# A four-layer network on one core: the last expert mixture as one stage, and the third attention's query rotation split

## The reference

```python
q_nope = (q_c @ W_uq)...            # q_c = q @ W_dq
q_rope = _rope(q_c @ W_qr)
scores = (einsum(q_nope, k_nope) + einsum(q_rope, k_rope)) * scale
scores = where((k_ids <= seg_id) & (k_ids >= seg_id - 8), scores, NEG)
attn = softmax(scores); out = (attn @ v) @ W_o
```

```python
scores = sigmoid(xt @ gate_w.T)                  # 8 experts
top_scores, top_idx = top_k(scores, 2)
top_scores = 2.5 * top_scores / (top_scores.sum() + 1e-20)
y[e] = (silu(xt @ w1[e]) * (xt @ w3[e])) @ w2[e]  # hidden width 176
out = sum of the chosen two, weighted, + (silu(xt @ sw1) * (xt @ sw3)) @ sw2
```

## Time and profile before

| | us |
|---|---|
| median of 3 runs (2387.63 to 2402.3) | 2391.42 |
| the profiled execution | 2387.03 |
| its span | 2385.2 |
| third attention, first rotary add to the last tile | 747.4 to 1231 |
| gate, first DMA issue | 1997.4 |
| routing | 2033 to 2057 |
| scatters | 2058.6 to 2139.3 |
| first routed unit | 2157.1 |
| first read of the results (L3018) | 2341.9 |
| PE, DVE, ACT, POOL busy, share of the span | 81%, 66%, 41%, 50% |

### The profile page before, as it was taken

One profiled execution on the slowest core, in us unless ns is written; L12 is line 12 of the kernel. 1 busy time (PEld: TensorE's weight loads), 2 busy tenths in 40 slices (PEclk: granted clock), 3 DMA queues, 4 the chain that ended last, 5 costly groups with the idle time before them and its releaser, 6 DMA issues. The chain is left out here.

```text
span 2385.2 us, 46698 instructions
## 1 busy us (share of the span) xinstructions
PE 1920.2 (81%) x16094; PEld 1429.0 (60%) x16128; DVE 1568.5 (66%) x3473; ACT 984.2 (41%) x2503; POOL 1184.3 (50%) x1523
## 2 busy tenths in 40 slices
PE   6979744796914888888868996799999997379995
PEld 5869421674714777777756664366666663247773
DVE  7956721765596999999955455688788873533336
ACT  3732311242234555555532222376666664123331
POOL 4720046532384666666642323388777872362331
PEclk8989756898966999999989998699999998679997
DMA  7721055505650000000000000444444433132336
GB/s 208 250 65 48 10 162 125 182 6 145 80 143 1 0 0 0 0 0 0 0 1 1 1 1 7 119 107 107 102 105 104 108 76 83 47 107 75 107 107 227
DMA packets 155592, 179.90 MB, mean 75 GB/s; under 512 B 39452, under 2 KB 136908, under 8 KB 150796
## 3 DMA queue, kind: packets, MB, share of 16 engines
q1 hardware_dynamic: 145596, 155.33, 24.4%
q0 software_dynamic: 9808, 22.20, 3.1%
HBM read 117.55 MB, written 59.33 MB: 74 GB/s over the span
## 5 line engine op out<-in xcount | busy, mean ns | idle before, releaser
L2712 DVE TENSOR_REDUCE mx<-bank 128x2 f32<-128x512 f32 x512 | 321.4, 680 | 91.2 <-PE bank L2574 91.1
L2678 ACT ACTIVATE e<-bank 128x512 f32<-128x512 f32 x512 | 269.5, 606 | 136.5 <-PE bank L2594 136.4
L2506 POOL TENSOR_TENSOR es<-e 128x256 f32<-128x256 f32 x384 | 271.2, 729 | 92.6 <-ACT e L2678 92.0
L2574 PE MATMUL bank<-k,q 72*128 72x256 bf16 x1024 | 205.4, 285 | 33.7 <-DMA k<-k_parts 33.5
L1859 POOL TENSOR_TENSOR q_l<-q_l,rot_l 64x512 f32<-64x512 f32 x128 | 162.3, 1268 | 127.6 <-DVE rot_l L2056 127.6
L2594 PE MATMUL bank<-q,k 74*128 74x256 bf16 x1024 | 196.8, 276 | 6.2 <-DMA q<-rows 3.6
L2574 PEld LDWEIGHTS bank<-k,q 72*128 72x128 bf16 x1024 | 92.4, 100 | 95.7 <-issue 48.5
L2611 PE MATMUL bank<-e,val 128*32 128x256 f32 x2048 | 140.5, 392 | 3.1 <-ACT nd L2673 0.6
L3036 POOL DMA_INDIRECT y<-y,got x71 | 69.0, 972 | 130.9 <-DVE y L3152 125.8
L3081 PE MATMUL bank<-w,hT 88*128 (+1 forms) x412 | 112.8, 398 | 24.3 <-ACT hT L3106 24.3
L1891 PE MATMUL bank<-qcT,wq_abs 96*128 96x128 f32 x1024 | 124.0, 280 | 0.0
(11 more groups left out here) (433 smaller groups left out, 5115.4 us busy)
## 6 DMA issues: line engine op xcount, KB each, us to landing
q<-q_parts SPq DMA_DIRECT2D x32, 576.0 KB
k<-k_parts SPq DMA_DIRECT2D x96, 192.0 KB
got<-rows SPq DMA_DIRECT2D x71, 128.5 KB, 2.1
rows<-no_row SPq DMA_DIRECT2D x1, 9088.0 KB
moe_rows<-zero_a SPq DMA_DIRECT2D x16, 512.0 KB, 3.2
w<-in_e0w SPq DMA_DIRECT2D x16, 512.0 KB, 3.6
parts_y<-y SPq DMA_DIRECT2D x32, 256.0 KB, 4.6
k_parts<-k_parts_a SPq DMA_DIRECT2D x96, 64.0 KB, 2.1
```

The lines of the kernel that those rows point to most:

```text
L2506: nc.gpsimd.tensor_tensor(es[:, n, :], e[:, n, 0, :], e[:, n, 1, :], ALU.add).then_inc(s["sum_ready"], 1)
L2574: last = nc.tensor.matmul(scores(r)[:, qt * D:(qt + 1) * D], q[0:R, b, h * D + qt * P:h * D + qt * P + P], k[0:R, b, h * D:(h + 1) * D], s ...
L2678: nc.scalar.activation(e[:, slot(i, r), :, :].rearrange("p k n -> p (k n)"), scoresT(r)[:, :], ACT.Exp).then_inc(s["exp_ready"], 1)
L2712: v.tensor_reduce(mx[:, a.n, 0, at:at + 2], scores(r)[:, :].rearrange("p (a n) -> p a n", a=2), AX.X, ALU.max, negate=True).then_inc(s["ma ...
```

## The change

In the third attention, `q_ready` rises after each four heads, and `rope` can do some of the quarters: the first quarter of the next tile stands between the two `sums`, the other three behind the second. Those who need all heads wait for the fourth quarter.

In the think stage the fill of `rows3` goes, with its two buffers.

The last mixture becomes one stage, `stage_l3_moe`. The 24 shared units come in eight groups of three (PER = 3), and each group also carries four tiles through the gate and the routing. A tile is normalized once, into a ring of 20 buffers (RING = 5 groups); that buffer feeds both the transposes and both scatters, and ACT's second copy goes. PE adds the counts of a group by eight small bf16 matmuls (`rank`), and a running `base` on DVE takes the place of the scan. Each expert has an area of fixed place in `rows3` (AREA3 = 4224 rows), so a token's row is known once its group is counted. `choose` and `place` are 24 DVE instructions a group. After the last group, `tables` (20 instructions) works out the expert and the first row of each of the 71 row tiles. SP then stores one tile of padding at the end of each expert's area, at an address from a register. Each read of a row tile takes its address from a register too. Rows carry one more number, the lower of the token's two experts, and two small DVE instructions per routed unit work out the home in `y3`; the weights are worked out in `shares` before the routed units. SiLU and sigmoid now alternate on ACT within one block. The weights are loaded with the shared expert's first.

```diff
@@ stage_l1_think
-        no_row = sb("no_row", [P, D]); no_home = sb("no_home", [P, T3])
...
-            sp.wait_ge(s["t_no_row"], 2)
-            empty = c.rows3.rearrange("(n p) d -> p n d", p=P)
-            sp.dma_start(empty[:, :, 0:D], no_row[:, :].unsqueeze(1).broadcast_to([P, T3, D])).then_inc(s["t_filled"], 16)
-            sp.dma_start(empty[:, :, D:D + 1], no_home[:, :].unsqueeze(2),
-                         allow_slow_non_contiguous=True).then_inc(s["t_filled"], 16)
...
@@ stage_l2_attention
                 for h in range(H2):
                     last = nc.tensor.matmul(bank(j, h // 4)[:, (h % 4) * P:(h % 4 + 1) * P], wq[:, h, :],
                                             qcT[:, j, :], start=True, stop=True)
-                last.then_inc(s["q_ready"], 1)
+                    if h % 4 == 3:
+                        last.then_inc(s["q_ready"], 1)
...
-            def rope(t, j):
-
-                dve.wait_ge(s["q_ready"], ready(t))
+            def rope(t, j, some=range(4)):
+
                 dve.wait_ge(s["scores_ready"], halves(t - LANES, 1))
-                for m in range(4):
+                for m in some:
+                    dve.wait_ge(s["q_ready"], quarters(t, m))
...
-                for n in range(2):
-                    sums(t, j, n)
-                rope(t + 1, 1 - j)
+                sums(t, j, 0)
+                rope(t + 1, 1 - j, range(1))
+                sums(t, j, 1)
+                rope(t + 1, 1 - j, range(1, 4))
                 back(t, j)
@@ stage_l3_moe, the SP queue
+            sp.dma_start(wg[:, :, :], c.d["g3w"].rearrange("(k p) n -> p k n", p=P)).then_inc(s["g3_loaded"], 16)
...
+            sp.wait_ge(s["w3_loaded"], 96)
+            sp.wait_ge(s["tables_ready"], 1)
+            for e in range(E3):
+                at = nc.values_load(base_i[0:1, e:e + 1], engines=(mybir.EngineType.SP,), min_val=0, max_val=E3 * AREA3 - P)
+                sp.dma_start(c.rows3[bass.ds(at, P), :], pads[:, e, :]).then_inc(s["pads_out"], 16)
+            sp.wait_ge(s["spare_out"], 32)
+            sp.wait_ge(s["pads_out"], 16 * E3)
+            for j in range(RING):
+                sp.wait_ge(s[sent_out[j]], 16 * TOP3 * WIDE * len(range(j, GR, RING)))
             for n in range(T3):
+                at = nc.values_load(at_row_i[0:1, n:n + 1], engines=(mybir.EngineType.SP,), min_val=0,
+                                    max_val=E3 * AREA3 + (SPARE - 1) * P)
                 wait(sp, y_out[n % GOT], 16 * (n // GOT))
-                sp.dma_start(got[:, n % GOT, :], c.rows3[n * P:(n + 1) * P, :]).then_inc(s[got_in[n % GOT]], 16)
+                sp.dma_start(got[:, n % GOT, :], c.rows3[bass.ds(at, P), :]).then_inc(s[got_in[n % GOT]], 16)
@@ GpSimd
+            for i in range(GR):
+                pool.wait_ge(s["sent_ready"], i + 1)
+                for t in tiles(i):
+                    for k in range(TOP3):
+                        nc.gpsimd.indirect_dma_start(
+                            out=c.rows3[:, :], out_offset=bass.IndirectOffsetOnAxis(ap=pos3[:, t, k:k + 1], axis=0),
+                            in_=sent[:, slot(t), :], in_offset=None, oob_is_err=True, bounds_check=E3 * AREA3 - 1,
+                        ).then_inc(s[sent_out[i % RING]], 16)
@@ TensorE
+            early_features(0)
+            early_features(1)
+            logits(0)
+            turn_scores(0)
+            pe.wait_ge(s["w3_shared"], 48)
+            for u in range(FIRST):
+                i, m = u // PER, u % PER
+                if m == 0 and i + 2 < GR:
+                    early_features(i + 2)
+                hidden(u)
+                if m == 1 and i + 1 < GR:
+                    logits(i + 1)
+                if u >= 1:
+                    turn(u - 1)
+                if m == 1:
+                    rank(i)
+                if m == 2 and i + 1 < GR:
+                    turn_scores(i + 1)
+                if u >= 2:
+                    down(u - 2)
+            turn(FIRST - 1)
+            down(FIRST - 2)
+            pe.wait_ge(s["w3_loaded"], 96)
+            pe.wait_ge(s["tables_ready"], 1)
@@ ScalarE
+            for u in range(FIRST):
+                i, m = u // PER, u % PER
+                if m == 0 and i + 2 < GR:
+                    early_copies(i + 2)
+                sigmoid(u)
+                if m == 1 and i + 1 < GR:
+                    score(i + 1)
+                if u >= 1:
+                    copy(u - 1)
@@ VectorE
+            for u in range(FIRST):
+                i, m = u // PER, u % PER
+                product(u)
+                if m == 0:
+                    choose(i)
+                if m == 1:
+                    place(i)
+                if m == 2 and i + 3 < GR:
+                    norms(i + 3)
+                if u == FIRST - 1:
+                    tables()
+                if u >= 2:
+                    finish(u - 2)
+            finish(FIRST - 2)
+            shares()
```

More of the change, by code:

```diff
@@ L2757, in _, with stage_l3_moe @@
             stats(end)
[L2760 removed]
+def stage_l3_moe(nc, c):
     with ExitStack() as ctx:
         sb = lambda n, sh, dt=F32: ctx.enter_context(nc.sbuf_tensor(n, sh, dt))
[L2764 to L2783, removed]
[L2784 to L2862 removed]
@@ L2982, in stage_l3_experts @@
         gates = lambda u: c.bank[u % 2]
-        turned = lambda u: c.bank[2 + u % 2][0:HH3, 0:2 * P]
+        turned = lambda u: c.bank[2 + (u % 2 if u > FIRST else 0)][0:HH3, 0:2 * P]
+        out = lambda u: c.bank[6 + u % 2 if u >= FIRST else 7][:, 0:D]
+        early = lambda t: c.bank[4 + t % 2][:, 0:D]
         feat = lambda n: c.bank[4 + n % 2][:, 0:D]
-        out = lambda u: c.bank[6 + u % 2][:, 0:D]
+        logitsT = c.bank[6][0:E3, :]
+        scores = c.bank[3][:, 0:WIDE * E3]
+        counts = c.bank[3][:, 64:64 + (WIDE + 1) * E3].rearrange("p (a e) -> p a e", e=E3)
+        slot = lambda t: t % (RING * WIDE)
+        tiles = lambda i: range(WIDE * i, WIDE * i + WIDE)
+        some = lambda i: slice(WIDE * i, WIDE * i + WIDE)
         ot = c.d["out"].rearrange("(n p) d -> p n d", p=P)
@@ L3064, in turn @@
                 pe.wait_ge(s["hid_ready"], u + 1)
-                wait(pe, "hT_ready", u - 1)
+                wait(pe, "hT_ready", u if u <= FIRST else u - 1)
                 for n in range(2):
@@ L3097, in _, with early_copies, score @@
         def _(act):
+            def early_copies(i):
+                for t in tiles(i):
+                    act.wait_ge(s["feat_read"], t + 1)
+                    act.copy(xT3[:, t, :], early(t)).then_inc(s["feat_copied"], 1)
+            def score(i):
+                act.wait_ge(s["logit_ready"], i + 1)
+                wait(act, "score_turned", i - 1)
+                nc.scalar.activation(scoreT[:, i % 2, :], logitsT, ACT.Sigmoid).then_inc(s["score_ready"], 1)
             def sigmoid(u):
@@ new lines, in norms, with choose @@
+            def norms(i):
+                if i >= RING:
+                    dve.wait_ge(s[sent_out[i % RING]], 16 * TOP3 * WIDE * (i // RING))
+                for t in tiles(i):
+                    v.tensor_scalar(sent[:, slot(t), 0:D], c.x[:, t, :], c.mean[:, t:t + 1], c.rstd[:, t:t + 1],
+                                    ALU.subtract, ALU.mult).then_inc(s["xn_ready"], 1)
+            def choose(i):
+                dve.wait_ge(s["score_turned"], i + 1)
+                ch.link(v.tensor_copy(cand[:, some(i), 0:E3], scores.rearrange("p (t e) -> p t e", e=E3)))
+                for t in tiles(i):
+                    last = v.max(top[:, t, :], cand[:, t, 0:E3])
+                ch.link(last)
+                ch.link(v.memset(top[:, some(i), TOP3:8], BIG))
+                for a, t in enumerate(tiles(i)):
+                    last = v.match_replace(out=left[:, a, :], in_to_replace=top[:, t, :], in_values=cand[:, t, :],
+                                           imm_value=-BIG)
+                ch.link(last)
+                v.tensor_tensor(mask_b[:, i % 2, :, :], left[:, :, 0:E3], cand[:, some(i), 0:E3],
+                                ALU.not_equal).then_inc(s["chosen_ready"], 1)
+                ch.link(v.tensor_tensor(mask[:, some(i), :], left[:, :, 0:E3], cand[:, some(i), 0:E3], ALU.not_equal))
```

427 lines of the change are left out of this document (198 added, 229 removed).

## The result

| | before | after |
|---|---|---|
| median of 15 runs each, us | 2391.63 (2386.21 to 2402.3) | 2409.08 (2402.2 to 2417.52) |
| ratio to before, 95% interval | | 1.0072, 1.0057 to 1.0086 |
| profiled execution, us (span) | 2387.03 (2385.2) | 2405.14 (2403.3) |

The change costs 17.5 us where 20 us less were forecast. The time lies beyond the range too. The mixture gained what was promised, and a little more; the attention lost three times what was promised.

A forecast was written before the change was run, and what follows sets the result against it. One core, barriered stages; in the third attention PE and DVE, each 88% busy, share the limit. Mixture -39, attention +19, fill 0 make -20 us: from 2391.4 to a forecast of 2371 us, 8-in-10 range 2345 to 2400.

The forecast's parts named there:

- Second sum and second turn: Third attention: their starts, forecast at 2.17 and 4.26 us after T0, the end of the first half's reciprocal.
- Nothing among them shrinks: turn to scores stays 5.90 us: Third attention, PE: second turn, both reads, projection and next scores keep their old pace, so scores start at T0+10.16.
- First half's scores: Third attention: 32 matmuls of about 1.1 us plus 0.1 hand-over to DVE, so the mask starts at T0+11.36.
- Mask to sum: Third attention: 3.22 us from mask to first exponent's end, so the first sum starts at T0+14.60; step 15.50 us.
- The bounds of the attention, -20 to +28: Around +19 us: -20 if PE's later turn is fully hidden, +28 if nothing is, with 0.3 us more latency per step.
- rival (c): Mixture: merged loop stays slow on PE's clock, slower by over 1% from a 17 us group; chance 0.11.
- Quarter signals: Third attention: signalling by quarters costs three more semaphore events on PE; no time was counted for them.
- The fill: Think stage: removing the 9.3 MB fill counts 0 us, with bounds 0 and -3 us.
- The front of the mixture: Mixture, stage start to first routed matmul: 159.7 us shortened by 39, bounds -45 and -31, at 11.6 us a group.
- the 3 us for it: Mixture: PE, idle some 15 us, starts the routed units at the lower clock level, costing 3 us.
- Rival (a): Third attention: rotation free through the projection's 1.4 us slack (chance 0.14), or gaining 0.66 us per step (0.10).
- Table loads bind: Mixture: ACT's two added table loads per group, 1.28 us each, forecast as hidden, would set the pace; chance 0.12.

The follow-up runs named there:

- e4: The changed kernel with seven more matmuls on PE in each attention step, in the gap before the second turn; 2398.54 us, 0.9952 of before.
- e3: The changed kernel with only DVE's old order put back (both sums, then the four rotations), quarter signals kept; 2365.79 us, 0.9820 of before.
- e6: The kernel before, unchanged, run again for a second profile; the median of before in its group was 2395.42 us.
- e5: The kernel after, unchanged, run again in another group; 2407.76 us, 1.0053 of before.
- e7: The changed kernel with only one of the first quarter's three rotation instructions between the two sums; 2324.45 us, 0.9707 of before.
- e10: e7 with SiLU in place of the sigmoid in the mixture's routing score; no total time given, its mixture front takes 132.6 us.
- e9: The changed kernel with two of the first quarter's three rotation instructions between the two sums; 0.9901 of before.
- e8: The changed kernel with the last four heads of the next tile's queries moved into PE's gap before the second turn; 2373.48 us, 0.9919 of before.
- e2: The changed kernel with the attention's functions of before; 2367.74 us, 0.9842 of before.
- e12: e7 once more, unchanged, in a later group; 2349.93 us, 0.9754 of before.

## Why the prediction was wrong

Term by term, with the forecast's numbers first.

- **Second sum and second turn**, T0+2.17 and 4.26: 2.18 and 4.27. Right.
- **"Nothing among them shrinks: turn to scores stays 5.90 us"**: 7.24. This is the step that failed. The durations of before were taken as fixed, but they were those of a PE that sat idle for 0.42 us before that turn, at a grant near 1 (0.98 over the stage, 1.00 from 790 to 1190). The edit's own delay made a hole of 2.00 us, and the turn and reads behind it ran at grants of 0.50 and 0.63. That is 1.34 us a step, 40 us in all. e4, with the hole filled, shows the 5.90 again.
- **First half's scores, 1.20 us to the mask**: 1.39 (1029.42 to 1030.81). Another 0.19, 6 us.
- **Mask to sum**, 14.60 - 11.36 = 3.24 us: 1034.04 - 1030.81 = 3.23. Right. With 1.34 and 0.19 on top of 15.50 the sum gives 17.03; this step is 17.05 (1034.96 - 1017.91).
- **The bounds of the attention, -20 to +28**: the upper one allowed 0.3 us of latencies and no change of clock, so the measured +63 was outside. Even the upper bound, with the mixture as measured, would have given a time inside the range. The forecast did treat the clock, as rival (c), but in the mixture, where the grant was low already (0.70), and not in the attention, where it was 0.98 and the change was about to make a hole.
- **Quarter signals**, nothing: nothing (e3).
- **The fill**, 0: from the first norm of the think stage to the first of the attention it is 174.8 us in before and 172.4 in after, 174.3 in e6 and 176.5 in e5. Right.
- **The front of the mixture, -39**: -45 in the first profiles (159.7 to 114.3). A full group of four tiles took 11.04 us, not 11.6, so the loop's last product ended 91.8 us into the stage, not 98.3; the allowance of 0.5 for handovers and the count matmuls at 0.9 were too dear (eight of them take about 0.35 us together, 2099.21 to 2099.56 in the trace of after). The tables took 6.2 (5.6), SP's stores 8.5 (8.0), the read 2.1 (2.1), and from the last product to the first routed matmul it was 22.5 us (19.3). No row shows the forecast's 0.2 us of register arithmetic by itself; a register and its store together took 1.06 us each, where 0.99 was counted. The first routed unit does start slowly: its first four matmuls take 2.71 us at a grant of 0.50, where they took 1.35 in before. Before shows the same at the start of its shared units, where PE had idled for 15.03 us and eight such matmuls took 5.03 us, at a grant of 0.50 up to 2062. Yet the 3 us for it are not seen in the sum: from its start to the end it is 227.6 us, and 228.1 in before.
- **Rival (a)**: fell for this change; the projection is late, not early, and DVE waits 2.22 us for it. It came true in e7.
- **"Table loads bind"**, 0.12 of the chances: fell by e10. A load has a mean of 1283 ns in after, and no cost beyond it is seen: the load of 2099.92 starts 0.02 us behind the copy before it, and the SiLU behind the load waits 0.55 us for PE's bank.
- **Rival (c)**: fell. The merged loop had a grant of 1.00, with PE busy 74.9 of 76.5 us.

That +63 - 45 = +18 meets the measured difference so well is in part luck. Stages in which no line was changed moved too: ahead of the think stage after is 7.0 us later than before (its first norm at 569.7 and 562.7), and from the first norm behind the third attention to the mixture's first transfer it is 6.9 us shorter (754.2 and 761.1). The two cancel. Over all profiles that first norm lies at 562.7 to 573.2 us, and the second stretch takes 752 to 765 us, in before's second profile 754.7. So a single profile leaves some 7 to 13 us open in stages that nobody touched; why is open. The +63 and -45 are read inside their own stages.

## What to carry to other kernels

Before you price a delay by old durations, look at what TensorE does while it waits: if the edit opens an idle stretch like the 1.3 to 2.0 us here in front of matmuls on the critical cycle, price those at up to twice their time as one bound, an estimate from the grant of 0.50 behind the hole in after, where the turn took 1.11 us for 0.66 (1.27 us of idling cost the full price in 8 steps of 26 of e9, 2.00 in every complete step of after), and compare the cost of filling the stretch with work you have anyway. And size what you slip in between two links of a chain by the wait that is there: 0.71 us in a wait of 0.66 won 0.5 us a step, 2.14 us in the same wait lost 2.1. And read more than one step before you name a small cost: the 0.28 us in the reads of one step is in before as well.

## What the runs showed of the hardware that was not expected

- In the step of after shown above, TensorE's loss of clock shows mostly behind the hole: the grant is 0.91 during the 2.00 us of idling, 0.50 in the 1.02 us after, 0.63 in the next 2.70, then 1.00.
- The same pause can cost the full price or nothing. In e9, behind 1.27 us of idling before the second turn, turn to scores is 5.90 us in 17 of 26 steps, 7.39 to 7.46 in 8 and 6.18 in one. Behind 1.54 and 1.11 us it is 5.90 in 21 of 24 steps (e8, longest 6.17), behind 0.44 us in 24 of 25 (e4), and behind 0.43 to 0.57 us in 26 of 27 (e7).
- Work without any use, 1.7 us of it per step on an engine busy 85% (338 of 400 us in after, 790 to 1190), shortened the step from 17.0 to 15.8 us (e4).
- In seven kernels of the first and third group (e2, e3, e4, e9 to e12) DVE stood still for 20 to 25 us in the merged loop in front of one instruction, seven or six times, up to 4.6 us, with no releaser in the trace. The second group (e5, e7, e8), with the same kernel as e12 among it, and after's first profile show nothing of it.
